# A shared tile moved ahead of the eighth expert group, one attention tile moved to VectorE, and a low-rank product taken in high and low parts

## The chip, the cores and the metric

The kernel runs on one core of a Trainium2 chip. The metric is the device time of one execution in microseconds (us); lower is better. TensorE is written PE, VectorE DVE, ScalarE ACT, GpSimd POOL and SyncE SP, as in the profile.

## What is computed

Two transformer layers over x of shape (4, 256, 256), 1024 tokens of width 256, all in 32-bit floats. Each layer adds an attention part and an FFN part, both taken of the same normalised input:

```python
xn = _layernorm(x)
x = x + L0_attn(xn) + L0_ffn(xn)
xn = _layernorm(x)
x = x + L1_attn(xn) + L1_ffn(xn)
```

The first layer's attention is causal with 16 heads of 128. Its FFN is a dense product plus a low-rank mixture of experts; the low-rank part is

```python
xa = einsum('ni,eri->ner', x_flat, A)      # 16 experts of rank 16
wxa = xa * coeff[:, :, None]               # top-2 of 16
delta = einsum('ner,eor->no', wxa, B)
out = x_flat @ W.T + bias + delta
```

The second layer's attention runs over the batch axis: the sequence is the 4 batch rows, causal, with 16 heads of 16 and 4 key/value heads, so a token attends to at most 4 others. Its FFN has 32 experts, top-4, at most 32 tokens each, of inner width 176, and a shared expert of inner width 704:

```python
shared = silu(x @ Wsg) * (x @ Wsu) @ Wsd
shared = shared * sigmoid(x @ Wse)
```

## The kernel before

Tokens are handled in 8 tiles of 128. Most products take each operand as a rounded high part and the rest of it, the low part; `mm3` (L1029) issues three products, high by low, low by high and high by high. The high part is a copy on ACT, the low part a subtraction on DVE. Products on unsplit 32-bit floats are one `pe.matmul` that the profile shows as two instructions.

**First layer.** PE fills the queries, then loops over 64 units (a head of one batch row; L1277). A unit is scores, a turn of the probabilities and the heads' product, with a piece of the key and value projections between; from unit 58 on the first pieces of the layer's output stand there. DVE takes the maxima, ACT the exponentials and the copies, POOL the query parts and the normalisation. Beside this ACT and DVE split other weights: `wo_high` (L854) and `wo_low` (L1748) split the output weights, 128x512 at a time, at units 22, 23, 30, 31 and 58 to 62. Behind the units comes the output loop over tiles (L1292 to L1304): `out_heads`, a turn of the normalised tile, `qkv`, and `out_small(j, 0)` and `out_small(j, 1)` (L1234) for the dense and the low-rank product. The latter is the two plain products of L1244, WXT by B2.

**Second layer.** Here the order of the work is the hand-written list EXPERT_STEPS (L33 to L43), which PE, ACT and DVE each walk, every one doing its own share of a step. `("up", g)` is the up product of expert group g (8 groups of 4 experts; PE L1408, ACT L992, DVE L2019), `("turn", g)` a transpose (L1418), `("down", g)` the down product (L1428) with its weighting (ACT L971, DVE L1986), `("merge", g)` a product that sums rows of the same token (L1436) and `("copy", g)` its copy (ACT L975). `("sd", j)` is tile j of the shared expert's down product on PE: j 0 and 1 are plain products (L1452), j 2 and on are `mm3` (L1450, L1454) and wait for the splits `("split", n)` (ACT L1016, DVE L2045 for n 1 to 6; from tile 4 on all of them) and, for the PSUM bank, for `add_shared(j - 2)` on DVE (L1996), which DVE reaches in step `("sd", j - 1)`. `("weighed", n)` normalises the attention's probabilities on DVE (L1888). `("ao", h)` turns half h of the attention's values on PE (L1469), with the high part on ACT (L1024) and the low part on DVE (L2030).

The attention's values of a tile j are j // 2 + 1 products of 128x256 with a sum behind each but the first. Tiles 0 to 5 are POOL's (`values`, L685), in the list PV_STEPS (L62), between the indirect scatters of merged expert rows (L703); tiles 6 and 7 are DVE's (`last_values`, L1968), in steps `("values", n)`.

SP's queue loads the expert weights in order (L543 to L555): each group's up weights, 1.4 MB, go to one of 4 places once the group four before has used it (`s_up`), each group's down weights, 0.7 MB, likewise (`s_dn`). The last ones are asked for in the order up 6, down 5, up 7, down 6, down 7. Behind them SP reads back the scattered rows (L559) and stores the output (L562). PE ends with `final_tile` for 8 tiles (L1496), DVE with two sums for each (L1992, L2002).

## Time and profile before

| | us |
|---|---|
| runs | 421.21, 423.23, 422.12 |
| median of the runs | 422.12 |
| the profiled execution's own time | 419.93 |
| its span | 418.2 |
| PE busy | 409.2 |
| DVE busy | 317.1 |
| ACT busy | 251.2 |
| POOL busy | 176.4 |

The profiled execution is 0.5% below the median of the runs, and 1.7 us of its time lie outside the span. A row of a timeline gives the start of an instruction (or of several like it), how long it took, and in brackets how long its engine had been idle before and what ended that.

### The profile page before, as it was taken

Reading aid. Unit: us, or ns where it says so; the run is one execution under the profiler, and the core shown is the slowest. Engines: PE = TensorE matmul, PEld = TensorE weight load, DVE = VectorE, ACT = ScalarE, POOL = GpSimd, SP = SyncE. Lnnn points to the kernel's source line nnn. Section 1 sums busy time; section 2 is a strip of 40 time slices with the busy share of each in tenths; the row PEclk is TensorE's granted clock in tenths of the full one; section 3 lists DMA queues with packets and bytes.
Section 4 is the critical chain, followed back from the end, with each engine's and each line's share of the span. In section 5 each row is a group of like instructions: output and inputs, shape, how many; then the busy total and the mean of one; then the engine's idle time right before and its main releaser. Section 6 shows DMA issues by size and latency. Waiting matters only on the chain.

```text
span 418.2 us, 8765 instructions
## 1 busy us (share of the span) xinstructions
PE 409.2 (98%) x2986; PEld 366.3 (88%) x2986; DVE 317.1 (76%) x926; ACT 251.2 (60%) x682; POOL 176.4 (42%) x298
## 2 busy tenths in 40 slices
PE   8999999999999999999999999999999999996997
PEld 7888889999999999999999999999999877553897
DVE  5867675787787888887777777665588998688846
ACT  3757651896868878787868688433424623673510
POOL 4440002655454554545555531011145603777860
PEclk9999999999999999999999999999999999999999
DMA  7960011601010101001000000000049940699364
GB/s 212 312 231 1 2 59 44 202 1 52 2 51 2 52 2 46 7 0 54 2 0 2 2 0 2 15 25 14 14 161 394 347 175 25 243 352 336 50 168 152
DMA packets 23788, 39.84 MB, mean 95 GB/s; under 512 B 2560, under 2 KB 19264, under 8 KB 22976
## 3 DMA queue, kind: packets, MB, share of 16 engines
q1 hardware_dynamic: 22352, 37.31, 26.1%
q0 software_dynamic: 1392, 1.97, 2.5%
q8 instruction: 25, 0.41, 0.4%
q14 instruction: 19, 0.16, 0.1%
HBM read 33.90 MB, written 5.37 MB: 94 GB/s over the span
## 4 chain that ended last, share of the span: by engine, by line
PE 91%; DMA 5%; DVE 2%; SPq 0%; ACT 0%; issue 0%; DVEq 0%
PE bank L1031 23%; PE bank L1032 23%; PE bank L1033 23%; PE bank L1202 5%; DMA arena<-in_experts_up 4%; PE bank L1214 3%; PE bank L1193 3%; PE bank L1244 2%; DMA X<-in_L_attn_x 1%; PE bank L1408 1%; PE bank L1428 1%; PE bank L1352 1%; PE bank L1452 1%; PE bank L1070 1%; PE bank L1062 0%; PE bank L1222 0%
## 5 line engine op out<-in xcount | busy, mean ns | idle before, releaser
L641 POOL TENSOR_TENSOR arena<-arena,rinv 128x384 f32<-128x384 f32 x64 | 53.0, 828 | 81.0 <-DVE rinv L1727 81.0
L1031 PE MATMUL bank<-XTl,WA 128*128 128x512 f32 (+1 forms) x126 | 51.9, 412 | 0.1
L1033 PE MATMUL bank<-XTh,WA 128*128 128x512 f32 (+1 forms) x126 | 49.2, 390 | 0.0
L1032 PE MATMUL bank<-XTh,WA 128*128 128x512 f32 (+1 forms) x126 | 49.1, 390 | 0.0
L845 ACT ACTIVATE PT<-bank 128x256 fp32r<-128x256 f32 x64 | 24.5, 383 | 34.0 <-PE bank L1202 34.0
L1731 DVE TENSOR_TENSOR PT<-bank,PT 128x256 fp32r<-128x256 f32 x64 | 27.2, 425 | 18.8 <-ACT arena L846 18.8
L1031 PE MATMUL bank<-WA,XTh 128*128 128x256 f32 x128 | 38.3, 299 | 0.0
L632 POOL CAST Q<-arena 128x128 fp32r<-128x128 f32 x64 | 18.7, 292 | 45.2 <-PE bank L1033 45.2
L1032 PE MATMUL bank<-WA,XTl 128*128 128x256 f32 x128 | 35.7, 279 | 0.0
L1033 PE MATMUL bank<-WA,XTh 128*128 128x256 f32 x128 | 35.7, 279 | 0.0
L1719 DVE CUSTOM_DVE_ANT_0 arena<-bank,posm 128x128 f32<-128x128 f32 x64 | 18.1, 283 | 20.9 <-PE bank L1033 20.9
L838 ACT ACTIVATE arena<-arena,nmax 128x256 f32<-128x256 f32 x64 | 32.3, 505 | 0.0
L634 POOL TENSOR_TENSOR Q<-arena,Q 128x128 fp32r<-128x128 f32 x64 | 29.7, 464 | 5.1
L1202 PE MATMUL bank<-ident,arena 128*128 128x128 f32 x192 | 31.4, 272 | 0.0
L851 ACT ACTIVATE arena<-bank,VC 128x256 f32<-128x256 f32 x64 | 30.0, 469 | 0.1
L1033 PEld LDWEIGHTS bank<-XTh,WA 128*128 128x128 f32 x126 | 23.7, 188 | 5.3
L1031 PEld LDWEIGHTS bank<-XTl,WA 128*128 128x128 f32 x126 | 23.8, 189 | 4.4 <-issue 0.5
L1032 PEld LDWEIGHTS bank<-XTh,WA 128*128 128x128 f32 x126 | 23.8, 189 | 3.8
L754 ACT ACTIVATE arena<-bank,bqs 128x512 f32<-128x512 f32 x16 | 18.5, 1154 | 14.5 <-PE bank L1033 13.6
L1721 DVE CUSTOM_DVE_ANT_0 arena<-bank,posm 128x256 f32<-128x256 f32 x64 | 26.9, 420 | 0.0
L836 ACT ACTIVATE arena<-arena,nmax 128x128 f32<-128x128 f32 x64 | 25.9, 404 | 1.6 <-DVE nmax L1721 1.1
L625 POOL TENSOR_TENSOR arena<-arena 128x256 f32<-128x256 f32 x20 | 15.4, 796 | 27.0 <-ACT arena L905 22.5
(362 smaller groups left out, 1453.2 us busy)
## 6 DMA issues: line engine op xcount, KB each, us to landing
arena<-in_experts_up SPq DMA_DIRECT2D x6, 1408.0 KB, 10.1
arena<-in_experts_down SPq DMA_DIRECT2D x6, 512.0 KB, 9.3
expert_rows<-arena SPq DMA_DIRECT2D x2, 1152.0 KB, 11.9
arena<-in_L_attn_Wk SPq DMA_DIRECT2D x8, 256.0 KB, 2.6
arena<-in_L_attn_Wv SPq DMA_DIRECT2D x8, 256.0 KB, 3.3
arena<-in_L_attn_Wo SPq DMA_DIRECT2D x1, 2048.0 KB, 8.3
arena<-expert_rows SPq DMA_DIRECT2D x8, 256.0 KB, 3.5
XT<-in_experts_up SPq DMA_DIRECT2D x2, 704.0 KB, 7.6
```

What stands on the lines that cost most here:

```text
L634: pool.tensor_tensor(QL[:, u % 3], q, QH[:, u % 3].bitcast(F32), ALU.subtract).then_inc(s_qh, 1)
L641: pool.tensor_tensor(pr, pr, r[:, :, None].to_broadcast([P, 3, P]), ALU.mult).then_inc(s_p, 1)
L836: nc.scalar.activation(Pb[i][:, 0:128], Pb[i][:, 0:128], ACT.Exp, bias=nmax[:, i, 0:1], scale=-1.0, accum_out=psumr[:, i, 0:1])
L838: nc.scalar.activation(Pb[i][:, 128:384], Pb[i][:, 128:384], ACT.Exp, bias=nmax[:, i, 1:2], scale=-1.0, accum_out=psumr[:, i, 1:2]).then_i ...
L845: nc.scalar.activation(PTH[:, u % 2], pb[2 + u % 2][:, 0:256], ACT.Copy)
L851: nc.scalar.activation(QO[:, h, b], pb[4 + u % 2][:, 0:256], ACT.Identity, bias=VC[:, 32 + h:33 + h]).then_inc(s_Oc, 1)
L1031: pe.matmul(dst, wh, xl, start=start, stop=False)
L1032: pe.matmul(dst, wl, xh, start=False, stop=False)
L1033: return pe.matmul(dst, wh, xh, start=False, stop=stop)
L1202: ins = pe.transpose(pb[2 + u % 2][:, P * i:P * i + P], Pb[u % 3][:, P * i:P * i + P], ident[:])
L1721: nc.vector.tensor_tensor_reduce(Pb[i][:, 128:384], bank[:, 128:384], MASK, -1.0, -MASKED, ALU.add, ALU.min, nmax[:, i, 1:2]).then_inc(s_m, 1)
L1731: nc.vector.tensor_tensor(PTL[:, u % 2], pb[2 + u % 2][:, 0:256], PTH[:, u % 2].bitcast(F32), ALU.subtract).then_inc(s_Tl, 1)
```

## The change

- EXPERT_STEPS: `("sd", 1)` stands ahead of `("up", 7)`, and the tiles behind it follow one place earlier each; `("values", n)` has six steps, with tile 5's first, and they and the splits are spread anew; `("weighed", 0)` is gone from the list, and DVE does it in step `("shared", (8, 1))`.
- PV_STEPS: POOL keeps the values of tiles 0 to 4; the last three scatters have nothing between them.
- The low-rank product is `mm3` of WXT's and B2's high and low parts. The splits are new work for ACT (`rows_split`) and DVE (`rows_low`): B2 (128x512) and four tiles of WXT (128x256 each) behind units 38, 39, 46, 47 and 54, and two pairs of tiles (128x512 each) in step 0 of the output loop.

The diff:

```diff
@@ -32,15 +32,16 @@
 EXPERT_STEPS = [("table", 0), ("shared", (8, 1)), ("shared", (9, 0)), ("shared", (9, 1)), ("weigh", 0), ("shared", (10, 0)), ("shared", (10, 1)),
                 ("slots", 0), ("shared", (11, 0)), ("shared", (11, 1)), ("slots", 1)]
-EXPERT_STEPS += [("up", 0), ("slots", 2), ("up", 1), ("weighed", 0), ("turn", 0), ("slots", 3),
+EXPERT_STEPS += [("up", 0), ("slots", 2), ("up", 1), ("turn", 0), ("slots", 3),
                  ("up", 2), ("ranks", 0), ("down", 0), ("turn", 1), ("slots", 4), ("weighed", 1),
                  ("up", 3), ("merge", 0), ("copy", 0), ("down", 1), ("split", 0), ("turn", 2), ("slots", 5),
                  ("up", 4), ("merge", 1), ("copy", 1), ("down", 2), ("proj", 0), ("split", 7), ("turn", 3), ("slots", 6), ("mask", 0),
-                 ("up", 5), ("merge", 2), ("copy", 2), ("down", 3), ("split", 8), ("turn", 4), ("slots", 7), ("split", 9), ("sd", 0), ("values", 0), ("split", 1),
-                 ("up", 6), ("merge", 3), ("copy", 3), ("down", 4), ("split", 2), ("turn", 5), ("values", 1),
-                 ("up", 7), ("merge", 4), ("copy", 4), ("down", 5), ("turn", 6), ("split", 3), ("sd", 1), ("values", 2),
-                 ("merge", 5), ("copy", 5), ("down", 6), ("split", 4), ("turn", 7), ("sd", 2), ("values", 3), ("merge", 6), ("copy", 6),
-                 ("down", 7), ("split", 5), ("ao", 0), ("sd", 3), ("split", 6), ("ao", 1), ("sd", 4), ("sd", 5), ("sd", 6), ("sd", 7), ("add", 7)]
+                 ("up", 5), ("merge", 2), ("copy", 2), ("down", 3), ("split", 8), ("turn", 4), ("slots", 7), ("split", 9), ("values", 0), ("sd", 0),
+                 ("split", 1), ("values", 1),
+                 ("up", 6), ("merge", 3), ("copy", 3), ("down", 4), ("split", 2), ("turn", 5), ("values", 2), ("sd", 1), ("split", 3),
+                 ("up", 7), ("merge", 4), ("copy", 4), ("down", 5), ("turn", 6), ("split", 4), ("values", 3), ("sd", 2),
+                 ("merge", 5), ("copy", 5), ("down", 6), ("split", 5), ("values", 4), ("turn", 7), ("sd", 3), ("merge", 6), ("copy", 6), ("split", 6),
+                 ("values", 5), ("down", 7), ("ao", 0), ("sd", 4), ("ao", 1), ("sd", 5), ("sd", 6), ("sd", 7), ("add", 7)]
 AHEAD = 6
 E0, RANK, HID = 16, 16, 64
 H1, D1, G1 = 16, 16, 4
@@ -61,7 +62,10 @@
 FINAL_BANK = (1, 4, 5, 6, 0, 2, 7, 3)
 PV_STEPS = [("values", (0, 0)), ("values", (1, 0)), ("scatter", 0), ("values", (2, 0)), ("values", (2, 1)), ("scatter", 1),
             ("values", (3, 0)), ("values", (3, 1)), ("scatter", 2), ("values", (4, 0)), ("values", (4, 1)), ("scatter", 3),
-            ("values", (4, 2)), ("scatter", 4), ("values", (5, 0)), ("values", (5, 1)), ("scatter", 5), ("values", (5, 2)), ("scatter", 6)]
+            ("values", (4, 2))] + [("scatter", g) for g in range(4, LAST)]
+PV = 13
+DVE_VALUES = [(5, (0, 1)), (5, (2,)), (6, (0, 1)), (6, (2, 3)), (7, (0, 1)), (7, (2, 3))]
+SPLIT_AT = (38, 39, 46, 47, 54)
 IN_FRONT = {2: 0, 3: 1, 4: 2, 5: 3, 6: 4, 7: 6}
 MASKED = -1.0e30
@@ -159,6 +163,9 @@
         TW = nc.alloc_sbuf_tensor_at("TW", [P, NT, TC], FR, offset=at_lg)
         WXT = region(33792, 2048).rearrange("p (c n) -> p c n", c=C)
+        WXTl = nc.alloc_sbuf_tensor_at("WXTl", [P, C, N], FR, offset=at0 + 4 * 33792)
+        B2h = nc.alloc_sbuf_tensor_at("B2h", [P, C, D], FR, offset=at_lg)
+        B2l = nc.alloc_sbuf_tensor_at("B2l", [P, C, D], FR, offset=at0 + 4 * 31232)
         at1 = nc.sbuf_base
@@ -235,7 +242,9 @@
         SG = SG.rearrange("p (i s a c n) -> p i s a c n", i=2, s=2, a=2, c=C)
         DM = [DM[:, 0:N], DM[:, N:2 * N], FRX[:, 2944:2944 + N]]
         selb = sb("selb", [P, NT, E1], BF16)
+        at_sel = nc.sbuf_base
         sel = sb("sel", [P, NT, E1])
+        at_tmp1 = nc.sbuf_base
         tmp1 = sb("tmp1", [P, NT, E1])
         posm = sb("posm", [P, NT, E1])
@@ -254,7 +263,13 @@
         sig = sb("sig", [P, NT])
         mx1 = sb("mx1", [P, 2, 4 * H1])
         MXp = [mx1[:, :, 0:3 * H1], mx1[:, :, 3 * H1:4 * H1]]
+        at_pvt = nc.sbuf_base
         pvt = sb("pvt", [P, 256])
+        WXH = [R1T] + [nc.alloc_sbuf_tensor_at(f"WXH{i}", [P, C, P], FR, offset=at) for i, at in enumerate((at_pvt, at_sel, at_tmp1))]
+        WXH += [nc.alloc_sbuf_tensor_at(f"WXH{i}", [P, C, 2 * P], FR, offset=at0 + 4 * at) for i, at in ((4, 30208), (6, 33024))]
+
+        def rows_high(j):
+            return WXH[j] if j < 4 else WXH[4 + (j - 4) // 2][:, :, P * (j % 2):P * (j % 2) + P]
         onesr = sb("onesr", [1, P], FR)
         spare = sb("spare", [P, 1])
         silu_ready = sb("silu_ready", [P, 1])
@@ -873,6 +888,18 @@
                 nc.scalar.activation(o_place(n)[:, 0], QO[:, 8 * (n % 2):8 * (n % 2) + 8, j // 2, P * (j % 2):P * (j % 2) + P],
                                      ACT.Copy).then_inc(s_oh, 1)
+            def rows_split(n):
+                if n == 0:
+                    act.wait_ge(s_wxc, 4)
+                    weight_copy(B2h[:], B2, 5)
+                elif n < 5:
+                    j = n - 1
+                    nc.scalar.activation(WXH[j][:], WXT[:, :, P * j:P * j + P], ACT.Copy).then_inc(s_tc, 1)
+                else:
+                    at = 4 * P + 2 * P * (n - 5)
+                    act.wait_ge(s_O, UNITS)
+                    nc.scalar.activation(WXH[n - 1][:], WXT[:, :, at:at + 2 * P], ACT.Copy).then_inc(s_tc, 1)
+
             turned_copy(0)
             exps(0)
             exps(1)
@@ -891,6 +918,8 @@
                     wo_high(WO_AT.index(u))
                 if u in O_AT:
                     o_high(O_AT[u])
+                if u in SPLIT_AT:
+                    rows_split(SPLIT_AT.index(u))
                 if u % 8 in (2, 3) and u // 8 + 2 < PAIRS:
                     w_high_part(4 + u // 8 + 2, u % 8 - 2)
@@ -916,6 +945,9 @@
             for j in range(NT):
                 if 2 * j + 4 < 2 * NT:
                     o_high(2 * j + 4)
+                if j == 0:
+                    rows_split(5)
+                    rows_split(6)
                 if j >= 1:
                     t2_copy(j - 1)
                     if j == NT - 1:
@@ -1241,7 +1273,8 @@
                     if part == 0:
                         mm3(dst, XTh[:, c, t], XTl[:, c, t], WTh[:, c], WTl[:, c], c == 0, False)
                     else:
-                        pe.matmul(dst, WXT[:, c, t], B2[:, c], start=False, stop=False)
+                        pe.wait_ge(s_tl, 6 + j if j < 4 else 10 + (j - 4) // 2)
+                        mm3(dst, rows_high(j)[:, c], WXTl[:, c, t], B2h[:, c], B2l[:, c], False, False)
             def out_heads(n, part):
                 j, k = n // 2, n % 2
@@ -1462,8 +1495,8 @@
                 else:
                     pe.wait_ge(s_eh, GR)
                     pe.wait_ge(s_ec, GR)
-                    pe.wait_ge(s_pv, 18)
-                    pe.wait_ge(s_pd, 2)
+                    pe.wait_ge(s_pv, PV)
+                    pe.wait_ge(s_pd, 3)
                 for c in range(C):
                     for i in range(4):
                         ins = pe.transpose(pb[ao_bank(c, half)][:, P * i:P * i + P], AO[:, 4 * half + i, P * c:P * c + P], ident[:])
@@ -1756,6 +1789,13 @@
                 nc.vector.tensor_tensor(o_place(n)[:, 1], QO[:, 8 * (n % 2):8 * (n % 2) + 8, j // 2, P * (j % 2):P * (j % 2) + P],
                                         o_place(n)[:, 0].bitcast(F32), ALU.subtract).then_inc(s_ol, 1)
+            def rows_low(n):
+                if n == 0:
+                    weight_low(5, B2l[:], B2, B2h[:])
+                    return
+                at, size = (P * (n - 1), P) if n < 5 else (4 * P + 2 * P * (n - 5), 2 * P)
+                weight_low(5 + n, WXTl[:, :, at:at + size], WXT[:, :, at:at + size], WXH[n - 1][:])
+
             for u in range(UNITS):
                 if u + 2 < UNITS:
                     inverse_sums(u + 2)
@@ -1769,6 +1809,8 @@
                     wo_low(WO_AT.index(u - 1))
                 if u - 1 in O_AT:
                     o_low(O_AT[u - 1])
+                if u - 1 in SPLIT_AT:
+                    rows_low(SPLIT_AT.index(u - 1))
                 if u % 8 in (4, 5) and u // 8 + 2 < PAIRS:
                     w_low_part(4 + u // 8 + 2, u % 8 - 4)
@@ -1818,6 +1860,9 @@
                     xt_low(j - 1)
                 if 2 * j + 4 < 2 * NT:
                     o_low(2 * j + 4)
+                if j == 0:
+                    rows_low(5)
+                    rows_low(6)
                 if j == 6:
                     top_k_chosen(2)
                 if j == NT - 1:
@@ -1966,14 +2011,14 @@
                                                op0=ALU.add, op1=ALU.subtract).then_inc(s_rk, 1)
             def last_values(part):
-                j = NT - 2 + part // 2
-                for k in (0, 1) if part % 2 == 0 else (2, 3):
+                j, steps_of = DVE_VALUES[part]
+                for k in steps_of:
...
-                        if k == 3:
+                        if k == j // 2:
                             ins.then_inc(s_pd, 1)
                         else:
                             step(ins)
@@ -1988,7 +2033,7 @@
             def add_rows(j):
                 dve.wait_ge(s_x[j // 2], 32)
-                dve.wait_ge(s_pv, 18 + j + 1)
+                dve.wait_ge(s_pv, PV + j + 1)
                 step(nc.vector.tensor_tensor(X[:, j], YS[0][:, j], X[:, j], ALU.add))
             def add_shared(j):
@@ -2012,6 +2057,7 @@
                 if what == "shared" and n == (8, 1):
                     dve.wait_ge(s_sr, 9)
                     scores_less_max(1)
+                    scores_weighed(0)
                 if what == "shared" and n in ((9, 1), (10, 1)):
                     same_token(n[0] - 9)
                 if what == "up":
```

## Rows read from the trace of the kernel before

**Rows 1.** The page: busy time of each engine

```profile
PE 409.2 (98%) x2986; PEld 366.3 (88%) x2986; DVE 317.1 (76%) x926; ACT 251.2 (60%) x682; POOL 176.4 (42%) x298
...
```

**Rows 2.** All waits of PE (line, what it waited for: us, times, longest)

```profile
PE bank L1408 <- DMA arena<-in_experts_up: 3.2, 1, 3.2
...
PE bank L1031 <- DVE ACTl L2045: 0.4, 1, 0.4
...
```

**Rows 3.** Timeline of PE around the eighth up product

```profile
379.51 1.07 PE L1428 MATMUL bank<-arena 128*32 128x256 f32 x16
...
384.17 1.39 PE L1408 MATMUL bank<-arena 128*32 128x352 f32 x16 [3.22 <-DMA arena<-in_experts_up]
...
387.20 1.46 PE L1452 MATMUL bank<-FRF,arena 128*128 128x256 f32 x6
...
389.60 0.47 PE L1436 MATMUL bank<-YW,SAMEr 128*128 128x256 f32 x1
```

**Rows 4.** Timeline of SP's queue: the first and the eighth group's load

```profile
359.87 2.03 SPq L522 DMA_DIRECT2D arena<-in_experts_up  x2
...
369.25 0.33 SPq L522 DMA_DIRECT2D arena<-in_experts_up  x1
```

**Rows 5.** Windows: busy time by engine, then granted clock, DMA share, GB/s

```profile
359.87:384.17 24.30, 20.83 (x221) 10.38 (x221) 20.35 (x37) 13.90 (x41) 18.76 (x18) 1.00 0.99 347
```

**Rows 6.** Timeline of PE: the first mm3 tile behind all splits, and the final tiles

```profile
399.35 0.36 PE L1031 MATMUL bank<-SDl,ACTh 128*128 128x256 f32 x1 [0.37 <-DVE ACTl L2045]
...
407.86 0.28 PE L1031 MATMUL bank<-PJ,AOTh 128*128 128x256 f32 x1
```

**Rows 7.** The values on DVE: count, ns of one (min/median/max), first and last start

```profile
L1973 DVE TENSOR_TENSOR arena<-arena x8: 424/792/865, 377.6 to 394.4; 128x256 f32<-128x256 f32 x8
...
L1975 DVE TENSOR_TENSOR arena<-arena x6: 425/584/828, 379.4 to 394.8; 128x256 f32<-128x256 f32 x6
```

**Rows 8.** Timeline of DVE behind the eighth group's up product

```profile
387.57 0.48 DVE L1986 SCALAR_TENSOR_TENSOR YW<-bank,slot_w,YW 128x256 fp32r<-128x256 f32 x1 [1.26 <-ACT YW L971]
388.40 0.69 DVE L2045 TENSOR_TENSOR ACTl<-arena,ACTh 128x512 fp32r<-128x512 f32 x1 [0.35 <-ACT ACTh L1016]
...
399.21 1.29 DVE L2030 TENSOR_TENSOR AOTl<-bank,AOTh 128x512 fp32r<-128x512 f32 x2
```

**Rows 9.** Timeline of POOL: from the fifth scatter on

```profile
388.70 1.86 POOL L703 DMA_INDIRECT expert_rows<-arena,rank  x1 [0.28 <-POOL arena L693]
...
398.23 1.58 POOL L703 DMA_INDIRECT expert_rows<-arena,rank  x1 [0.61 <-POOL arena L693]
```

**Rows 10.** Timeline of PE: out_small of tile 3 and what follows it

```profile
279.88 1.02 PE L1244 MATMUL bank<-arena 128*128 128x256 f32 x4
...
280.86 0.28 PE L1032 MATMUL bank<-FRX,OS 128*128 128x256 f32 x1
```

**Rows 11.** Weight loads of L1244 and of an mm3 tile, columns as in 7

```profile
L1244 PEld LDWEIGHTS bank<-arena x32: 187/188/192, 246.7 to 297.6; 128*128 128x128 f32 x32
...
L1031 PEld LDWEIGHTS bank<-SDl,ACTh x24: 186/188/189, 399.3 to 407.4; 128*128 128x128 f32 x24
```

**Rows 12.** Lines L859 (wo_high) and L1751 (wo_low), columns as in 7

```profile
L859 ACT ACTIVATE FRX<-arena x4: 627/628/628, 143.4 to 169.4; 128x512 fp32r<-128x512 f32 x4
...
L1751 DVE TENSOR_TENSOR FRX<-arena,FRX x4: 682/682/683, 146.5 to 172.5; 128x512 fp32r<-128x512 f32 x4
```

**Rows 13.** Timelines of DVE and of ACT at the start of the output loop

```profile
264.93 0.42 DVE L1827 TENSOR_TENSOR X<-bank,X 128x256 f32<-128x256 f32 x1 [2.05 <-PE bank L1033]
...
266.25 0.20 ACT L927 ACTIVATE rstd<-mv 128x1 f32<-128x1 f32 x1 [3.52 <-DVE mv L1831]
```

**Rows 14.** Timeline of DVE around weighed(0)

```profile
355.05 0.69 DVE L1861 TENSOR_TENSOR WAF<-WAF,bank 128x512 f32<-128x512 f32 x1 [0.96 <-PE bank L1033]
...
357.95 0.69 DVE L1859 TENSOR_TENSOR arena<-arena,bank 64x512 f32<-64x512 f32 x1 [1.61 <-PE bank L1033]
...
362.76 0.75 DVE L1891 RECIPROCAL mx<-mx 128x96 f32<-128x96 f32 x1
```

## The prediction

> **What bounds the kernel now.** I read the busy times first, then the waits of PE, then the timelines around the places that these named. PE is busy for 409.2 of the 418.2 us, and no other engine for more than 76% [rows 1]. PE's waits are few: one of 3.2 us for a DMA of expert weights, one of 0.4 us for DVE [rows 2], and some at the start and below 0.4 us. So what counts is PE's own work, and those waits. The long one stands in front of the eighth group's up product: PE is through with group 4's down product at 380.58 and with the turn behind it at 384.17 - 3.22 = 380.95, and goes on at 384.17 [rows 3]. The loads behind it go out between 359.87 and 369.25 [rows 4], and until it ends the DMA engines are busy for 0.99 of the time at 347 GB/s [rows 5]. The weights come no sooner whatever PE does meanwhile; the granted clock stays 1.00 through the wait, so nothing is to be had there. Behind it PE is dense up to the 0.37 us in front of the first tile that needs all splits, at 399.35, and from there four tiles take until 407.86, 2.13 us each (18 products, so 0.118 us each); then come the final tiles [rows 6].
>
> **The shared tile ahead of the eighth group.** Tile 1 is moved from behind 387.20 into the wait. It takes 2.40 us (387.20 to 389.60 [rows 3]) and needs nothing that is not there: it uses no split, and its bank's last reader is long done. The wait is 3.22 us, so 0.8 us of it is left, the weights arrive when they did, and everything on PE behind them comes 2.40 us earlier. SP has no request between the two places of the tile (each waits on an up or a down product), so its queue is not moved. Take the start of tile 5 as the mark; it is now 399.35 + 2.13 = 401.48. Without tile 1's 2.40 and with DVE in time (the 0.37 us of [rows 6]), PE alone would be there at 398.7: a gain of 2.8.
>
> **The attention values.** DVE takes over tile 5: three products and two sums, each between 0.42 and 0.87 us [rows 7], 2.1 to 4.3 in all. Those come in steps 0 and 1, around 378 to 382, but push tiles 6 and 7 later, and those must be done before the second half's turn on PE. What is queued behind them on DVE is what PE waits for: tile 3 waits for the sum of tile 1, tile 4 for the last split, tile 5 for the sum of tile 3, which in DVE's order stands behind `values` 5, the low part of group 7 and the first half's two low parts. From 387.57, where DVE takes up group 5's low part (set by PE, unchanged), the way to that sum is: 3 low parts at 0.48, 3 splits at 0.69, 11 values at 0.43 (products and sums, 4 of tile 6 and 7 of tile 7), the two low parts at 1.29 together [rows 8], and 3 sums as long as a low part: 1.44 + 2.07 + 4.7 + 1.29 + 1.44 = 10.9 us. To that come waits for ACT, 0.35 in front of the first split [rows 8] and as much again twice, since the weighting of group 6 and the last split's copy follow PE: 1.1. So DVE is there at 399.6, and PE starts tile 5 at 399.7. The gain there is 401.48 - 399.7 = **1.8 us** of the 2.8. Its bounds: 2.8 if DVE is never late, and with all 11 values at the slow 0.83 instead of 0.43, 4.4 us more, a loss of 2.6. I take the fast price for this reason: the slow ones lie beside POOL's own work, and of what POOL did from 388.70 to 398.23 [rows 9] only the three scatters are left, while its values between them are gone.
>
> The fast and the slow price of the same instruction stand in [rows 7]. The Trainium skill (GPSIMD Engine Reference, Specifications) says that GpSimd's SBUF interfaces are shared with VectorE, with contention for VectorE instructions with two SBUF inputs, as these are. By that rule tile 5 on DVE is paid for partly by less contention; by a fixed price at the median the move would cost more.
>
> POOL itself loses five instructions, and its last two scatters start as soon as the merged rows are copied, the last of them some us before the 398.23 of now; the read-back and POOL's sums come earlier too. I cost this at nothing: PE's final tiles hide it. DVE's last two sums for a tile fit into a final tile of eight products, 0.94 us.
>
> **The low-rank product.** Two plain products take from 279.88 to the next one's start, 280.86 less 0.12: 0.86 us [rows 10]. Six products at the pace of [rows 6] take 0.71. Times 8 tiles: **1.2 us** less, all on PE's path. Bounds: as in [rows 6] for the gain; for a loss, the weight loads. A load takes 188 ns for either kind [rows 11]; four per tile now, six then. If loads did not overlap, six would take 1.13, and the change would cost 0.27 x 8 = 2.2 us. But [rows 6] are such a stream, one load and one product each 0.118 us, so I take 0.71.
>
> **The new splits.** Seven copies on ACT and seven subtractions on DVE, at most 0.63 and 0.68 us each (the 128x512 ones of [rows 12]; those of 128x256 are cheaper). I cost them at nothing. The cover is the lag of the unit loop: output-weight splits of that size stand at units 22, 23, 30 and 31, the new ones at 38, 39, 46, 47 and 54, the same places in the period of 8, and no wait of PE came of the old. In the output loop's step 0 ACT has 3.52 us idle and DVE 2.05 before tile 0's sum [rows 13], and two copies are 1.26, two subtractions 1.36. The slot for those on DVE is the tighter. The waits that PE gains (`s_tl`) come 4 units or more behind the splits.
>
> **The softmax's third step.** `weighed(0)` is three instructions of at most 0.75 us, 2.25 in all, and moves into 0.96 and 1.61 us of idle time on DVE [rows 14]. What is queued behind it, a shared product and `same_token`, has PE ask for it only some us later. It frees POOL about 1 us earlier at the values of tile 0, and scatter 0 waits for a merge anyhow. Nothing.
>
> **The sum.** 1.2 + 1.8 = 3.0 us. Against the profiled execution: span 415.2, time 416.9. It stood 2.2 us below the median of the runs; from 422.12 the forecast is **419.1**, 0.7% less. About 0.5%, 2.1 us, is what a measurement of this kernel can tell from no change.
>
> **Rivals.**
> - *DVE takes the tail's gain.* If the four values of tile 6 behind the eighth group keep to the median 0.79 of [rows 7], DVE is 1.5 us later and the tail gives 0.3: 420.6. For it: DVE is nearly without a pause there already. Against: POOL falls idle from about 390.6. Chance 0.24.
> - *DVE is never late.* 1.2 + 2.8: 418.1. It needs all its waits for ACT to shrink; 0.08.
> - *The splits are not covered (slower).* Where: units 38 to 54, decided when a unit's spare time on ACT and DVE together is below the pair of 1.31 us. Then PE waits for the turned probabilities. Price: 5 x 1.31 = 6.6, less 3.0: 425.7. The earlier splits speak against it [rows 12]; DVE has only 24% idle. Chance 0.06.
> - *Loads bind.* The product would cost 2.2 instead of gaining 1.2: 422.5. For it: loads are busy for 88% of the span [rows 1], and the change adds 16 of them net. Against: the stream of [rows 6]. Chance 0.03. The Trainium skill (Trainium Kernel Development and Optimization, Best Practices) tells to judge PE's distance from its limit by the busy share of LDWEIGHTS and not by that of the matmuls; by that rule this rival, and not the 1.2, would be the outcome.
> - *The tile does not fill the wait*: the weights land later by what it took, because some load hangs on PE behind it. I find no such wait in SP's list. 1.2 only, 420.9. Chance 0.03.
>
> **How the numbers follow.** The forecast has 0.56. The low end of the range is the case without DVE's lateness, 418.1, less a part of the runs' spread (they lie 0.9 below to 1.1 above their median): 417.5. The high end takes in 420.6 and 420.9 with as much spread: 421.8. Loads and uncovered splits, 0.09, stay mostly outside. Faster by over 0.5% means below 420.0: 0.55 of the forecast's and the 0.08, so 0.63. Slower: 0.06 and a little of the loads' case, 0.07. The rest, 0.30, is the same.
>
> **What the profile after would show.** The wait for the up weights at about 1 us or below, with 12 plain products ahead of it; L1244 gone and 6 products of 0.118 us in its place; no new wait of PE between 100 and 300 us; DVE's products of values near 0.43 behind the eighth group; a wait of PE of 0.5 to 1.2 us in front of tile 5, for DVE's sum of tile 3. It is wrong if PE waits in the unit loop, if the up product still waits 3 us, or if the waits of the tail add up to over 2 us.

## The result and the profile after

| | before | after |
|---|---|---|
| median of the runs, us | 422.68 (421.21 to 423.52, 4 runs) | 417.39 (415.89 to 420.04, 4 runs) |
| ratio | 1 | 0.9879 [0.9851, 0.9906] |
| profiled execution, own time | 419.93 | 415.89 |
| its span | 418.2 | 414.2 |

The changed kernel is 5.1 us faster (4.0 to 6.3 by the interval), 1.2%. The forecast was 0.7%, and 417.39 lies 0.1 us below the low end of the range. The two profiled executions, on the other hand, differ by 4.0 us, and the forecast's sum was 3.0. So there are two questions: what the 4.0 us are made of, and why the medians differ by still more. (Three runs further below took 670 us and more, in a state of their own, and count in no ratio.)

The page of the changed kernel, busy time of each engine (the answer to [rows 1]):

```profile
PE 408.1 (99%) x3002; PEld 365.8 (88%) x3002; DVE 320.3 (77%) x938; ACT 254.3 (61%) x689; POOL 171.2 (41%) x293
```

PE has 16 more instructions (48 fp32r products for 32 records of plain ones) and is busy for 1.1 us less. DVE has 3.2 us more and POOL 5.2 us less. The waits of PE, those of the output loop's and the expert part's lines (the answer to [rows 2]; what is left out are the start and two waits of 0.3 us or less):

```profile
PE bank L1063 <- DVE X L2041: 0.6, 2, 0.4
PE bank L1441 <- DMA arena<-in_experts_up: 0.4, 1, 0.4
...
PE bank L1441 <- issue: 0.3, 1, 0.3
```

The 3.2 us for the up weights are down to 0.4. Nothing new stands between 100 and 300 us. The timeline of PE at the places of [rows 3] and [rows 6]:

```profile
378.94 1.46 PE L1485 MATMUL bank<-FRF,arena 128*128 128x256 f32 x6
...
382.07 1.39 PE L1441 MATMUL bank<-arena 128*32 128x352 f32 x16 [0.38 <-DMA arena<-in_experts_up]
...
389.21 0.39 PE L1063 MATMUL bank<-SDl,ACTx 128*128 128x256 f32 x1 [0.18 <-DVE X L2041]
...
397.28 0.39 PE L1063 MATMUL bank<-SDl,ACTh 128*128 128x256 f32 x1 [0.37 <-DVE X L2041]
...
403.80 0.29 PE L1063 MATMUL bank<-PJ,AOTh 128*128 128x256 f32 x1
```

Tile 1 (L1485) now stands ahead of the up product. The mark of the prediction, the start of tile 5, is the row at 397.28, with the forecast kind of wait in front of it, for DVE's sum of tile 3. The final tiles follow at 403.80.

With these marks the 4.0 us of the two profiles divide so:

| stretch, ended by | before | after | gained in it |
|---|---|---|---|
| start to the turn of unit 59's probabilities | 245.17 | 244.67 | 0.50 |
| to group 0's up product | 358.43 | 356.87 | 1.06 |
| to group 7's up product | 384.17 | 382.07 | 0.54 |
| to the start of tile 5 | 401.48 | 397.28 | 2.10 |
| to the first final tile | 407.86 | 403.80 | -0.14 |
| to the end of the span | 418.2 | 414.2 | -0.06 |

The first stretch holds of the change only the splits behind units 38 to 54, and its 0.50 us is not theirs: in the profiles of before_again and after_again, described below, the same mark stands at 246.19 and 244.56, in those of wait_filled_with_dummies and values_back, with the first-layer code of before and after, at 245.47 and 245.43. The second holds the low-rank product, in the new form (PE, `out_small` of tile 3, the answer to [rows 10]):

```profile
278.79 0.28 PE L1063 MATMUL bank<-B2l,WXH 128*128 128x256 f32 x1
278.91 0.28 PE L1064 MATMUL bank<-B2h,WXTl 128*128 128x256 f32 x1
...
279.50 0.28 PE L1063 MATMUL bank<-FRX,OS 128*128 128x256 f32 x1
```

From 278.79 to the next product at 279.50 are 0.71 us, the forecast's figure to the digit, where two plain products took 0.86. Eight times 0.15 is 1.2, and 1.06 came; this stretch hardly varies, it is 113.19 to 113.26 us in three profiles with the plain product (before, before_again, wait_filled_with_dummies) and 112.16 to 112.21 in three with the new one (after, after_again, values_back). The third stretch is the stream of weight loads, which took 23.76 us from SP's request to the product (24.30 before [rows 5]), with the same share and rate as before:

```profile
358.31:382.07 23.76, 23.38 (x232) 12.57 (x232) 18.37 (x34) 14.42 (x42) 18.28 (x18) 1.00 0.99 347
```

In the fourth, the tail of the prediction, 2.10 us came where 1.8 was forecast. DVE behind the up product, whose pace set the forecast (the answer to [rows 8]):

```profile
385.47 0.48 DVE L2031 SCALAR_TENSOR_TENSOR YW<-bank,slot_w,YW 128x256 fp32r<-128x256 f32 x1 [0.30 <-ACT YW L1003]
386.31 0.74 DVE L2091 TENSOR_TENSOR ACTl<-WAF,ACTh 128x512 fp32r<-128x512 f32 x1 [0.35 <-ACT ACTh L1048]
386.97 0.41 DVE L2018 TENSOR_TENSOR arena<-arena 128x256 f32<-128x256 f32 x1
387.42 0.42 DVE L2020 TENSOR_TENSOR arena<-arena 128x256 f32<-128x256 f32 x1
...
392.84 0.69 DVE L2091 TENSOR_TENSOR ACTl<-arena,ACTh 128x512 fp32r<-128x512 f32 x1 [0.63 <-ACT ACTh L1048]
...
396.75 0.47 DVE L2041 SCALAR_TENSOR_TENSOR X<-bank,sig,X 128x256 f32<-128x256 f32 x1
```

The products and sums of the values take 0.41 to 0.43 us, the fast price. From 385.47 to the end of the sum at 397.22 are 11.75 us, against 10.9 + 1.1 = 12.0 forecast.

### The profile page after: what moved, and what is told of

Same layout as the page of the kernel before. It is cut to its first block, busy times and chain, and to the rows that moved or that the text cites. A ratio compares the mean times of both kernels' runs of the same rounds, so it can differ in the third digit from the quotient of the medians.

```text
span 414.2 us, 8817 instructions
## 1 busy us (share of the span) xinstructions
PE 408.1 (99%) x3002; PEld 365.8 (88%) x3002; DVE 320.3 (77%) x938; ACT 254.3 (61%) x689; POOL 171.2 (41%) x293
## 4 chain that ended last, share of the span: by engine, by line
PE 92%; DMA 4%; DVE 2%; ACT 1%; issue 1%; SPq 0%; POOL 0%; POOLq 0%; DVEq 0%
PE bank L1063 24%; PE bank L1065 24%; PE bank L1064 24%; PE bank L1234 5%; DMA arena<-in_experts_up 4%; PE bank L1246 3%; PE bank L1225 3%; PE bank L1441 2%; PE bank L1140 1%; PE bank L1385 1%; PE bank L1102 1%; PE bank L1461 1%; PE bank L1076 1%; PE bank L1094 0%; PE bank L1254 0%
## 5 line engine op out<-in xcount | busy, mean ns | idle before, releaser
L838 ACT ACTIVATE K<-bank,VC 128x512 fp32r<-128x512 f32 x32 | 22.0, 688 | 7.6 <-PE bank L1065 7.5
```

## The experiments

Each comparison has its own runs of the kernel before on the same chip, since chips differ: its medians were 424.60 (29 runs), 422.24 (17) and 424.66 (13). So ratios are compared, not times. "Clock" is the mean granted clock of PE over a run.

| kernel | comparison | median, us | ratio to before | clock of its runs |
|---|---|---|---|---|
| low_rank_alone | 1 | 423.23 | 0.9974 [0.9944, 1.0005] | mostly 0.992 to 0.996 |
| all_but_low_rank | 1 | 419.92 | 0.9892 [0.9870, 0.9914] | 0.996 to 1.000 |
| tile_alone | 1 | 424.85 | 1.0006 [0.9989, 1.0023] | 0.991 to 1.000 |
| tile_back | 1 | 422.99 | 0.9973 [0.9954, 0.9991] | 0.988 to 0.996 |
| before_again | 2 | 422.52 | 0.9989 [0.9965, 1.0014] | 0.991 to 1.000 |
| after_again | 2 | 416.90 | 0.9867 [0.9848, 0.9886] | 1.000 |
| values_back | 2 | 418.80 | 0.9909 [0.9892, 0.9926] | 0.999 to 1.000 |
| wait_filled_with_dummies | 2 | 419.86 | 0.9935 [0.9916, 0.9953] | 0.999 to 1.000 |
| loads_swapped_before | 3 | 421.22 | 0.9924 [0.9898, 0.9951] | 1.000 |
| loads_swapped_after | 3 | 418.20 | 0.9854 [0.9819, 0.9889] | 0.996 to 1.000 |
| pool_busy_again | 3 | 421.30 | 0.9941 [0.9906, 0.9976] | 0.996 to 1.000 |
| softmax_step_back | 3 | 419.64 | 0.9881 [0.9851, 0.9911] | 0.996 to 1.000 |

### The parts one by one

**low_rank_alone** is the kernel before with the low-rank product as `mm3` and its splits, nothing else:

```diff
-                        pe.matmul(dst, WXT[:, c, t], B2[:, c], start=False, stop=False)
+                        pe.wait_ge(s_tl, 6 + j if j < 4 else 10 + (j - 4) // 2)
+                        mm3(dst, rows_high(j)[:, c], WXTl[:, c, t], B2h[:, c], B2l[:, c], False, False)
```

> The kernel before with the low-rank product in three products and its splits, nothing else. Theory (the parts add): 8 tiles x (0.86 - 0.71) = 1.1 to 1.2 us less, so 0.997 of before; L1244's two products gone, PE still waits about 3.2 us for the eighth group's up weights, since the load stream moves along with PE. Rival (weight loads bind): 2.2 us more. Rival (splits not covered): up to 6.6 us more, with waits of PE in the unit loop.

**all_but_low_rank** is the changed kernel with that edit undone, splits and all.

> The kernel after with the plain low-rank product and without its splits. Theory: what is left of the change, 2.8 to 2.9 us in the profile (4.0 less 1.1), so 0.993 of before. Rival (the timed difference of 1.2% is more than the profile's 4.0 us because the product gains more in the timed runs): 1.5 us or less.

The first gains 0.26% or 1.1 us, with an interval that just reaches no change; the second gains 1.08%, 4.6 us, where 2.8 to 2.9 were expected. Their sum, 5.7 us, is the whole (0.9867 to 0.9879, or 5.1 to 5.6 us). So the low-rank product is worth its 1.1 us, and nearly all that was not forecast lies in the other part. The clock column says where to look: three of the four runs of all_but_low_rank stand at 1.000 (419.81 to 419.96), and against the two of before at 1.000 on that chip (421.89 and 422.07) they gain 2.1 us, where 1.8 was forecast for this part.

**tile_alone** is the kernel before with tiles 1 to 4 one place earlier; POOL keeps tile 5 of the values:

```diff
-                 ("up", 6), ("merge", 3), ("copy", 3), ("down", 4), ("split", 2), ("turn", 5), ("values", 1),
-                 ("up", 7), ("merge", 4), ("copy", 4), ("down", 5), ("turn", 6), ("split", 3), ("sd", 1), ("values", 2),
+                 ("up", 6), ("merge", 3), ("copy", 3), ("down", 4), ("split", 2), ("turn", 5), ("values", 1), ("sd", 1),
+                 ("up", 7), ("merge", 4), ("copy", 4), ("down", 5), ("turn", 6), ("split", 3), ("values", 2), ("sd", 2),
```

> The kernel before with each shared tile from 1 to 4 one place earlier, tile 1 in front of the eighth group's up product; POOL keeps the values of tile 5, and POOL's and DVE's values stay where they were. Theory (the tile fills the wait and the tail is bound by PE until POOL's last values are late): PE's wait for the weights falls from 3.2 to about 0.8 us, but the second half's turn waits for POOL's tile 5, done at 397.6 in the profile before, and the splits of DVE come as late as before: tile 4 starts at 399.35 less at most 0.5, so 0.5 to 1.5 us gained. Rival (the tile alone is the gain and the values are of no matter): 2.4 us or more.

**tile_back** is the changed kernel with each of these tiles one place later again, and all else of the change kept.

> The kernel after with each shared tile one place later again, as in the kernel before; values on DVE, low-rank and softmax as after. Theory (the tile is what earns the tail, the values only let it): the wait for the weights is back at about 2.8 us, and the kernel is 2.0 to 2.4 us slower than after, 1.6 to 2.0 us faster than before. Rival (the relief of POOL earns it): less than 0.8 us slower than after.

tile_alone is not faster at all (1.0006), and its three runs at a clock of 0.999 or more (422.77, 423.44, 424.85) are all slower than the two of before at 1.000. tile_back has the gain of the low-rank product and no more (0.9973, where low_rank_alone has 0.9974). Both expectations failed: 0.5 to 1.5 us were expected of tile_alone, and tile_back loses 4.0 to 4.5 us to the changed kernel by the ratios, not 2.0 to 2.4, though PE's wait for the up weights is only 1.3 us in its profile, not 2.8. Neither the tile on its own nor DVE's new list on its own pays; together they pay 4.6 us. The waits of PE in tile_alone say why:

```profile
PE bank L1031 <- DVE ACTl L2045: 2.7, 1, 2.7
...
PE bank L1408 <- DMA arena<-in_experts_up: 0.7, 1, 0.7
...
PE bank L1031 <- DVE X L1996: 0.5, 1, 0.5
```

The wait for the up weights did shrink to 0.7 us, and what PE won it lost again in one wait of 2.7 us for DVE's last split: PE asks for it earlier, and DVE, with its splits and values in the old places, is no earlier. The saved time must be saved on DVE as well. tile_alone leaves out two things at once, the new places of the splits and the values of tile 5 on DVE; the next run takes back the second alone.

**values_back** is the changed kernel with tile 5 of the values on POOL, in the old places between the scatters:

```diff
-            ("values", (4, 2))] + [("scatter", g) for g in range(4, LAST)]
+            ("values", (4, 2)), ("scatter", 4), ("values", (5, 0)), ("values", (5, 1)), ("scatter", 5), ("values", (5, 2)), ("scatter", 6)]
-DVE_VALUES = [(5, (0, 1)), (5, (2,)), (6, (0, 1)), (6, (2, 3)), (7, (0, 1)), (7, (2, 3))]
+DVE_VALUES = [(), (), (6, (0, 1)), (6, (2, 3)), (7, (0, 1)), (7, (2, 3))]
```

> The kernel after with the values of tile 5 on POOL again, between the last scatters as before; tile order, splits, low-rank and softmax as after. Theory (the tile alone earned nothing because the last values and splits came too late for it): PE waits 1.5 to 3 us in front of the second half's turn for POOL's last values, and the kernel is 1.5 to 3 us slower than after. Rival (in the tile-alone run it was the order of DVE's splits, not POOL's values): within 0.7 us of after.

It is 1.9 us slower than after_again on the same chip (418.80 to 416.90), although DVE has five instructions less. The expectation had the size right and the place wrong: PE does not wait for POOL's last values in front of the second half's turn. Without the values the tile and the splits still earn something: the clock of these runs is 0.999 to 1.000, and the ratio 0.9909. But against the runs of before at 1.000 (419.75, the middle one) only 0.95 us are left, the low-rank product's part, so by this comparison what they earn is the clock, and the tail gets shorter only with the values on DVE. A stretch of DVE's timeline in values_back:

```profile
388.48 0.96 DVE L2018 TENSOR_TENSOR arena<-arena 128x256 f32<-128x256 f32 x1
389.47 0.42 DVE L2020 TENSOR_TENSOR arena<-arena 128x256 f32<-128x256 f32 x1
389.93 0.77 DVE L2018 TENSOR_TENSOR arena<-arena 128x256 f32<-128x256 f32 x1
390.74 0.74 DVE L2020 TENSOR_TENSOR arena<-arena 128x256 f32<-128x256 f32 x1
```

and POOL's in the same time:

```profile
388.00 1.16 POOL L708 TENSOR_TENSOR arena<-arena,pvt 128x256 f32<-128x256 f32 x1
389.43 1.60 POOL L718 DMA_INDIRECT expert_rows<-arena,rank  x1 [0.28 <-POOL arena L708]
390.46 1.51 POOL L704 TENSOR_TENSOR arena<-arena 128x256 f32<-128x256 f32 x1
```

The same instructions take 0.42 us where POOL computes nothing and 0.74 to 0.96 beside POOL's products and sums (whose spans in the profile are rough). PE pays for it in front of the tiles, 2.2 us for DVE's sums where the changed kernel has 0.6 or less:

```profile
PE bank L1063 <- DVE X L2041: 2.2, 2, 1.3
```

**pool_busy_again** keeps the values on DVE and lets POOL do three products and two sums of the same size on scratch in the freed places, so that DVE's list is the changed one and only the neighbour differs:

```diff
+            def busy(k):
+                p, v = value_operands(5, k)
+                step(pool.tensor_tensor(pvt[:].rearrange("p (g r d) -> p g r d", g=G1, r=4), p, v, ALU.mult))
+                if k:
+                    step(pool.tensor_tensor(pvt[:], pvt[:], pvt[:], ALU.add))
```

> The kernel after, with POOL doing five products and sums of 128x256 in the places from which tile 5's were taken, into a scratch tile that nobody reads; DVE keeps the values of tile 5. Theory (POOL's work beside DVE's doubles the time of DVE's values, and that relief pays for tile 5 on DVE): DVE's values behind the eighth group's up product go from 0.42 to 0.6 to 0.9 us each, PE waits 2 to 4 us more for DVE's sums, and the kernel is 2 to 4 us slower than after, also slower than with the values back on POOL (418.8). Rival (DVE's values are slow for another reason, or POOL's work is of no matter): within 0.7 us of after.

It loses about half of the gain: 0.9941 [0.9906, 0.9976] against the changed kernel's 0.9879 and 0.9867 on other chips, 2.6 to 3.1 us. Against softmax_step_back, its neighbour on the same chip and nearly the changed kernel, it is 1.7 us by the medians (421.30 to 419.64), and though the two intervals just touch, the runs do not overlap (420.22 at the least, 420.01 at the most). So that it is slower is clear, and how much is known only to between 1.7 and 3.1 us. DVE's values are slow again (0.74 to 0.78 us, and one sum 1.25, where the changed kernel has 0.42), and PE waits for it, 2.0 us in all where softmax_step_back has 1.0:

```profile
390.28 0.78 DVE L2028 TENSOR_TENSOR arena<-arena 128x256 f32<-128x256 f32 x1
391.10 0.75 DVE L2026 TENSOR_TENSOR arena<-arena 128x256 f32<-128x256 f32 x1
...
395.60 1.25 DVE L2028 TENSOR_TENSOR arena<-arena 128x256 f32<-128x256 f32 x1
...
PE bank L1071 <- DVE X L2049: 1.6, 2, 1.2
...
PE bank L1071 <- DVE ACTl L2099: 0.4, 1, 0.4
```

Once POOL has only a scatter left, from 397.88 on, DVE's last four values take 0.42 us again. So what makes the move of tile 5 pay is not that POOL finishes earlier, but that DVE's own products and sums, with no such work of POOL beside them, take about half the time. By the Trainium skill (GPSIMD Engine Reference, Specifications) this is to be expected for VectorE instructions with two SBUF inputs; the runs add how much it is.

**softmax_step_back** is the changed kernel with `("weighed", 0)` in its old step.

> The kernel after with weighed(0) in its old place behind the second up product. Theory (it is hidden there as well, as the kernel waits for loads soon after): a wait of 0.25 us of PE for DVE at the first merge comes back, and the time is that of after within 0.4 us. Rival (it starts POOL's list 1 us later, and with it all scatters and values): 0.8 us or more slower.

0.9881 [0.9851, 0.9911] stands beside 0.9867 and 0.9879: by the ratios its worth, costed at nothing, is 0.1 to 0.6 us, which the interval, 1.3 us to either side, can't tell from nothing.

### The gain that was not in the sum

In the comparison of the result the changed kernel had three of four runs at a clock of 1.000. The profile of before stood at 1.00 throughout, but it is one execution, so before_again was run: the kernel before itself, without an edit.

> The kernel before itself, for a second profile of it. Ratio 1.000. What is asked: where its granted clock falls to half, if it does, and whether the up product's signal comes late in it too. Theory (the 3.2 us wait for the eighth group's weights costs more than its length, as the clock falls behind it in many executions): a mean clock below 1.000 in most timed runs. Rival (nothing but the wait): mean clocks as in the kernel after.

Its profiled execution shows what that first one did not. The windows behind PE's long wait (length, PE busy, granted clock, DMA share, GB/s), and the timeline of PE:

```profile
380.00:386.00 6.00, 3.05 (x36) 0.95 1.03 332
386.00:390.00 4.00, 3.40 (x22) 0.50 0.80 210
390.00:392.00 2.00, 2.00 (x18) 0.50 0.24 38
392.00:394.00 2.00, 2.00 (x11) 0.94 0.40 35
394.00:396.00 2.00, 2.00 (x23) 1.00 0.20 30
```

```profile
386.60 2.58 PE L1408 MATMUL bank<-arena 128*32 128x352 f32 x16 [3.55 <-DMA arena<-in_experts_up]
...
389.83 1.94 PE L1428 MATMUL bank<-arena 128*32 128x256 f32 x16
...
404.15 0.36 PE L1031 MATMUL bank<-SDl,ACTh 128*128 128x256 f32 x1 [0.16 <-DVE ACTl L2045]
```

PE stood idle for 3.55 us. The granted clock falls while it does (the window up to 386 has 0.95) and is 0.50, that is 1.2 of 2.4 GHz, until past 392. The up product takes 2.58 us where it took 1.39 [rows 3], the next down product 1.94 where one took 1.07. From the up product to the first tile that needs all splits are 404.15 - 386.60 = 17.55 us; in the profile of before it was 399.35 - 384.17 = 15.18 [rows 3, 6]. The half clock cost 2.4 us. (Its span is longer by 4.8 in all; 1.5 more is the stream of loads, 360.82 to 386.60, and 0.95 lies ahead of it.) Of the 27 runs of the kernel before on this chip three kept a clock of 1.000, and took 419.62 to 419.88; fifteen had 0.995 or 0.996 (median 422.2), nine 0.991 or 0.992 (median 423.0).

The test of the cause is **wait_filled_with_dummies**: the kernel before, in which PE turns the identity 24 times into a free bank ahead of the last up product. Nothing useful is done earlier.

```diff
                 if what == "up":
+                    if n == 7:
+                        pe.wait_ge(s_xe, 8)
+                        for _ in range(24):
+                            pe.transpose(pb[1][:, 0:P], ident[:], ident[:])
                     expert_up(n)
```

> The kernel before with 24 transposes of the identity into a free bank in front of the eighth group's up product, about 2.7 us of PE work that nothing reads; no other change. Theory (idle time of PE costs clock behind it): the wait that is left is below 1 us, the tiles behind it start as before, and the timed runs have higher mean clocks and are 1 to 2 us faster than before. Rival (only the length of the wait counts, and a busy PE gains nothing): 1.000, or slower where the dummies reach beyond the weights' arrival.

```profile
381.08 2.78 PE L1483 MATMUL bank<-ident 128*128 128x128 f32 x24
384.62 1.39 PE L1408 MATMUL bank<-arena 128*32 128x352 f32 x16 [0.75 <-DMA arena<-in_experts_up]
...
400.32 0.36 PE L1031 MATMUL bank<-SDl,ACTh 128*128 128x256 f32 x1 [0.42 <-DVE ACTl L2049]
```

```profile
380.00:386.00 6.00, 5.25 (x59) 1.00 1.03 330
386.00:390.00 4.00, 4.00 (x32) 1.00 0.76 180
```

The up product is no earlier (384.62; 384.17 in before), the clock stays 1.00, and the kernel is 0.65% faster (0.47 to 0.84 by the interval), 2.4 us against the median of the comparison, where 1 to 2 were expected: 419.86, the time of those runs of before that kept their clock. So the long wait has a price of its own on top of its length, and that is gone when PE has anything to do in it. The Trainium skill (TensorE: Matmul & The Clock Gate, Why this matters for your kernels) warns of gaps between bursts of TensorE for this reason; these rows agree.

**loads_swapped_before** takes the wait away in another manner, with an earlier load:

```diff
-            load_down(5)
             load_up(7)
+            load_down(5)
```

> The kernel before with two loads exchanged in SP's list: the eighth group's up weights in front of the sixth group's down weights. Theory (the stream of loads is bound by its bytes, and 0.7 MB at 347 GB/s are 2.0 us): PE's wait for the up weights falls from 3.2 to about 1.2 us, the clock no longer falls behind it, and the timed runs are 3 to 5 us faster, 0.989 to 0.993, at mean clocks of 1.000. Rival (the down weights then come late for the sixth group's down product): the wait only moves there, 0.997 to 1.003.

```profile
PE bank L1428 <- issue: 0.9, 1, 0.9
PE bank L1408 <- DMA arena<-in_experts_up: 0.8, 1, 0.8
PE bank L1469 <- POOL arena L693: 0.7, 1, 0.7
```

The long wait has gone and several short ones stand in its place; all seven runs have a clock of 1.000, and the kernel is 0.76% faster by an exchange of two lines. **loads_swapped_after** has the same exchange in the changed kernel, as a candidate that might beat both.

> The kernel after with the same exchange of loads. Theory: only the 0.4 to 0.5 us that PE still waits for the up weights can be won, and DVE's lateness at the fifth tile takes part of it: 0.0 to 0.5 us faster than after. Rival (down weights late): slower than after by 0.5 us or more.

Its profile has no wait for the last up weights left, and 0.9854 [0.9819, 0.9889] is the lowest ratio of all, but the interval holds those of the changed kernel (0.9867, 0.9879): no better version is shown.

**after_again**, the changed kernel once more beside before_again, closes the account:

> The kernel after itself, on the chip of these runs. Theory (the parts add, 1.1 us of the low-rank product and 4.6 of the tile with the values): 5 to 6 us less than before, 0.987, mean clocks nearer 1.000 than those of before. Rival (4.0 us, as the first two profiles): 0.9905.

All five runs keep a clock of 1.000 and have a median of 416.9. Against the runs of before at the same clock, 419.6 to 419.9, that is 2.7 to 3.0 us: the forecast's sum. (These runs of before are three, and may be the ones whose weights came soonest.) Against the median of before, 422.24, it is 5.3 us by the medians and 5.6 by the ratio; the other 2.5 or so is clock. The price of the half clock, taken in three ways, is each time 2.4 or 2.5 us: 17.55 against 15.18 us in two profiles; 422.24 against 419.75, the middle one of the runs of before at 1.000; and the dummies in the wait. That they agree so well is in part chance: the profile is of a run at 0.992, and such runs have a median 3.3 us above 419.75, while the median of 422.24 is that of runs mostly at 0.996, which spend about half as long at half clock. Only the dummies change nothing but what PE does in the wait, so the price rests on them, and by their interval it is 2.0 to 3.5 us.

### What stays open

In all eight profiles of comparisons 1 and 3, whichever kernel, PE waits another 1.8 us at the first turn of the expert part; in none of the six profiles of before, after and comparison 2 does it. The row in tile_back, and the granted clock behind it:

```profile
361.71 0.33 PE L1451 MATMUL bank<-ident,arena 128*128 128x128 f32 x1 [1.82 <-DVE arena L2065]
```

```profile
362.00:364.00 2.00, 2.00 (x23) 0.76 0.79 287
364.00:366.00 2.00, 2.00 (x21) 0.50 1.00 428
366.00:368.00 2.00, 2.00 (x20) 0.89 1.02 434
```

It comes with both lists, so it isn't the change's. It begins with the first up product: by its record this ends in tile_back at 358.20, but ACT takes up its output only at 360.97, and SP's first load goes out 4.15 us behind its start, where in before ACT follows after 0.06 us and SP 1.44 us behind the start. The runs of before on those two chips are 2.4 us longer (424.6 to 422.2), which would fit, but why these followers are late is not known. Nor does half clock follow it always: it does in three of the four profiles of comparison 1 and in none of comparison 3. So a run at 0.996 there may have lost its clock at this place and not at the up product, and the comparison of low_rank_alone and tile_back, whose clocks are like before's, says nothing of the clock at the up product. Nor is the wait for the up weights the only one that goes with a lower clock: in tile_alone's profile 0.7 us of it are left, yet eight of its 11 runs stand at 0.991 to 0.996. Its profile, one at 1.00, has the 1.8 us at the turn and the 2.7 us for DVE, and which of these its other runs lose the clock behind is not shown. Open too is why an execution of before falls to half clock and another, with nearly as long a wait, doesn't.

## Why the prediction was right, and where it failed

- **The sum of 3.0 us** is what the change brings at equal clock: 2.7 to 3.0 us (after_again against the runs of before at 1.000), and without the low-rank product 2.1 us on another chip.
- **The low-rank product, 1.2**: 1.06 in the profile, 1.1 in low_rank_alone; 0.71 us for six products, as taken. The 16 added weight loads cost nothing, so *loads bind* is out (low_rank_alone has 0.9974 [0.9944, 1.0005], and 2.2 us more would be 1.005), and with it the judgement by the busy share of the loads.
- **The splits, nothing**: no wait of PE between 100 and 300 us. In the output loop DVE has both pairs behind it with 0.69 us of idle time left in front of tile 0's sum, where it had 2.05 [rows 13]:

```profile
262.17 1.28 DVE L1658 TENSOR_TENSOR WXTl<-arena,WXH 128x512 fp32r<-128x512 f32 x2
264.14 0.43 DVE L1872 TENSOR_TENSOR X<-bank,X 128x256 f32<-128x256 f32 x1 [0.69 <-PE bank L1065]
```

- **The tile in the wait, 2.40 of 3.22**: filled, with 0.38 us left in place of 0.8. The 0.4 us between the two is the shorter stream of loads in this profile (23.76 for 24.30 us), which varies by itself: 24.10 in after_again, 25.78 in before_again.
- **The tail, 1.8 of 2.8, DVE as its limit**: 2.10 in the profile, with the forecast kind of wait in front of tile 5, for the sum of tile 3, but of 0.37 us, less than the 0.5 to 1.2 forecast. The fast price was right, and for the reason given: pool_busy_again, with POOL's work put back, gives 1.7 to 3.1 us away. What the prediction did not see is that the tile hangs on DVE's list: it took the tile's gain to come by itself with DVE only trimming it, and tile_alone gives 1.0006.
- **The step that failed** is "the granted clock stays 1.00 through the wait, so nothing is to be had there". The row said so for one execution. In 24 of 27 runs of before on one chip the mean clock was below 1, and in the profile of such a run it stood at half behind this very wait, which cost 2.4 us. That is, within the intervals, the whole difference between the forecast's 0.7% and the measured 1.2%. The hint lay in the table ahead of the prediction: the profiled execution was 0.5% below the median, at 419.93, below each of the three runs. The prediction noted it, and carried the difference of 2.2 us over to the kernel after unchanged, as if it had nothing to do with what the change removes. Since the wait is gone, the changed kernel has less of it: 1.0 us in after_again (416.90 to 415.94) and 1.5 in the result (417.39 to 415.89). With the 2.4 us of clock in it the sum would have been 5.4, against 5.1 by the ratio and 5.3 by the medians.
- *DVE takes the tail's gain* (420.6) was wrong in the changed kernel, but is what values_back and pool_busy_again show when POOL stays busy. *DVE is never late* (418.1) was nearer to the measured median than the forecast, for the wrong reason: DVE is still late by 0.37 us, and the time came from the clock.

## What to carry to other kernels

A wait of TensorE for a transfer, 3.2 to 3.6 us here, costs its length and in most executions of this kernel about 2.4 us more behind it, since the clock falls to half; before such a wait is called free because the data come no sooner, move work into it, and compare the profiled execution's time and clock with those of the other runs. When work is moved earlier on the engine that bounds the kernel, the engines that feed its next steps must be made earlier by as much, or the gain returns as one wait further on. A product or sum on VectorE of two operands in SBUF has two prices here, 0.42 us, and 0.75 and more beside GpSimd's products and sums, so work taken off GpSimd can pay although VectorE has to do it.

## What the hardware showed unexpectedly

- TensorE idle for 3.55 us was followed by more than 6 us at a granted clock of 0.50 (386 to past 392), though it was busy for nearly all of them; another profile of the same kernel kept 1.00 behind 3.22 us of idle time, and so did 3 of 27 runs. 24 dummy turns of the identity in the gap, 2.78 us, kept the clock at 1.00 in every run but one, that one at 0.999.
- Products and sums of 128x256 on VectorE took 0.41 to 0.43 us alone or beside a scatter and 0.74 to 1.25 us beside GpSimd's products and sums.
- The same stream of expert weights took 23.76, 24.30 and 25.78 us from the request to its use in three profiles (24.10 in a fourth), without a change in the order of the loads.
